# Causal attention and a top-1 GELU mixture in one block that goes chunk by chunk

## The chip, the cores and the metric

The kernel runs on one core of a Trainium2 chip, as one program. The metric is the device time of one execution in microseconds. A core has TensorE (PE in the profile: matrix products; its weight loads are shown as PEld), VectorE (DVE), ScalarE (ACT), GpSimd (POOL) and SyncE (SP), which here issues nearly all DMAs. The engines run independent instruction streams and meet only at semaphores. TensorE's granted clock is given as a share of 2.4 GHz; it has two levels, 1.0 and 0.5 (1.2 GHz). All data of the block that changes are float32 except two small mask operands in bfloat16. A float32 product is recorded as two matmul records with a weight load each, a transpose as one.

## The reference, cut to what matters

The network has four layers of attention-like mixing and feed-forward, on 4096 tokens (8 x 512) of 128 features, each as `x = x + f(layernorm(x))`. The change touches the third layer alone:

```python
def _L2_attn_ref(x, wq, bq, wk, bk, wv, bv, wo, bo):   # H = 64, one head
    q = x @ wq + bq
    k = x @ wk + bk
    v = x @ wv + bv
    w = jnp.einsum('bqh,bkh->bqk', q, k) * scale
    w = w + mask                                       # causal, -1e11 above the diagonal
    w = jax.nn.softmax(w, axis=-1)
    z = jnp.einsum('bqk,bkh->bqh', w, v)
    return z @ wo + bo

def _L2_ffn_ref(x, Wg, bg, W1, b1, W2, b2):            # E = 8 experts of 128
    logits = xf @ Wg + bg
    idx = jnp.argmax(softmax(logits), axis=-1)
    h = gelu(jnp.einsum('th,ehi->tei', xf, W1) + b1, approximate=False)
    y = jnp.einsum('tei,eih->teh', h, W2) + b2
    out = y of the chosen expert, per token
```

The eight sequences of 512 tokens (`B, S = 8, 512`) are independent in the attention; the experts work on each token alone.

## The kernel before, in words

`program` calls one function for each part, each in blocks of its own; all engines meet at the end of a block. The residual x stays on chip as `net.x`, 32 tiles of 128 tokens. A chunk is one sequence, four tiles (`TC = 4`). The third layer runs as a row of blocks:

- `normalise` (L72): sqrt of the variances, then per chunk VectorE normalises four tiles, TensorE turns them, ScalarE copies them to `net.xT`.
- `causal_attention` (L1942): eight loads on SP's queue (L1980); GpSimd adds the output bias to all of x (L1996). The chunk loop is skewed over three chunks by `skewed` (L133): copy of the tokens (L2087), queries (L2008) and keys (L2012) as one product each into one PSUM tile with a copy after each (L2090), values (L2018), four causal rows of scores (L2029), on VectorE mask, maximum and scaling per row (L2124 to L2128), exponential with its sum on ScalarE (L2099), ten transposes of probabilities (L2039) with copies (L2134), the weighted sum with the turned probabilities as weights and the values moving (L2048), division by the sums (L2144), transposes of z (L2067), one more copy, projection (L2072) and the sum into x (L2152).
- `measure` (L156): mean and variance of all 32 tiles.
- `normalise_and_route` (L172): norm, turn, logits for all chunks. Then the choice for all tokens at once (`first_best`, L286) in a block of its own.
- `top1_gelu_products` (L2158): for each chunk the one-hot choice is turned (L2195) and copied twice (L2246, L2247). Expert e gets, before its product (L2207), a product of a mask (L2204) that adds -1e30 where the token has not chosen it, so that the gelu (L2259) gives zero; the down products of all experts and the bias of the chosen one accumulate in PSUM (L2216, L2218). Four PSUM banks `hps` hold up products, and the down products of chunk c-1 stand between those of chunk c. VectorE adds the output (L2268) and measures the tiles for the next layer.

The next layer, `decay_and_mlp` (L2301), is already one block in which steps s overlap the stages of several chunks by an order written out for each engine.

## Time and profile before

| | us |
|---|---|
| median of three runs | 1733.59 (1729.91 to 1737.28) |
| the profiled execution, its own time | 1743.69 |
| its span | 1741.9 |
| TensorE busy in the span | 1396.7 (80%) |
| VectorE busy | 986.0 (57%) |
| ScalarE busy | 788.3 (45%) |
| GpSimd busy | 504.4 (29%) |
| mean granted clock of TensorE | 0.856 |

The span is cut into stages by the blocks above: what an engine does in one of them stands in a window of the trace, not in these totals. A row of the timeline gives the start, the duration, the engine and line, what it writes and reads, and how many instructions are merged; brackets give the idle time before it and who ended it. The profile drops digits from names, so that the causal attention's tiles appear as `a_...`.

### The profile page before, as it was taken

To read this page: it belongs to the slowest core of one execution; us is meant where nothing else is said; L and a number is where in the kernel's file an instruction comes from. 1 tells how busy PE (TensorE), PEld (TensorE's weight loads), DVE (VectorE), ACT (ScalarE), POOL (GpSimd) and SP (SyncE) were. 2 spreads that over 40 slices of the span, in tenths; PEclk is the share of its full clock that TensorE was granted. 3 is DMA by queue.
4 is the path that set the end of the run, shared out by engine and by line. 5 is a ranking of instruction groups with operands and counts; after the bars stand their busy time and mean duration, and the time that the engine had idled before them with its cause. 6 is when DMAs were issued, how large, how long until landed. Compare 5 with 4: busy or idle time off the path is not lost. (4 is left out here: it accounts for less than half of the span.)

```text
span 1741.9 us, 22681 instructions
## 1 busy us (share of the span) xinstructions
PE 1396.7 (80%) x6994; PEld 787.8 (45%) x6994; DVE 986.0 (57%) x2717; ACT 788.3 (45%) x1600; POOL 504.4 (29%) x675
## 2 busy tenths in 40 slices
PE   5899999999952398357998895788589995999587
PEld 1233333333222297123655564355436664777432
DVE  7778888888446565389778533343520014555345
ACT  2567777777730154465664422322043322455344
POOL 4344244432100342855534432100000001321056
PEclk6899999999975599567999897776589996999889
DMA  5111111111052022102243240000000000000001
GB/s 149 41 49 48 43 38 50 53 47 29 11 161 45 20 60 46 33 14 50 51 84 64 50 98 5 0 1 0 1 25 1 1 1 18 1 1 1 2 30 31
DMA packets 75336, 63.24 MB, mean 36 GB/s; under 512 B 19131, under 2 KB 63372, under 8 KB 75220
## 3 DMA queue, kind: packets, MB, share of 16 engines
q1 hardware_dynamic: 71887, 56.13, 13.2%
q0 software_dynamic: 2304, 4.72, 1.1%
q8 instruction: 56, 0.92, 0.2%
q10 hardware_dynamic: 1028, 0.98, 0.2%
q14 instruction: 61, 0.49, 0.1%
HBM read 47.57 MB, written 13.79 MB: 35 GB/s over the span
## 5 line engine op out<-in xcount | busy, mean ns | idle before, releaser
L1060 DVE TENSOR_REDUCE a_nm<-a_aps 128x1 f32<-128x512 f32 x512 | 333.7, 687 | 74.7 <-PE a_aps L825 74.7
L1024 ACT ACTIVATE a_prob<-a_sps 128x512 f32<-128x512 f32 x512 | 271.5, 597 | 114.1 <-PE a_sps L837 113.2
L825 PE MATMUL a_aps<-a_K,a_Q 96*128 96x512 bf16 x512 | 195.6, 402 | 12.6 <-DMA a_K<-k_parts 12.3
L837 PE MATMUL a_sps<-a_Q,a_K 99*128 99x512 bf16 x512 | 156.6, 385 | 1.2 <-ACT a_prob L1024 1.2
L1529 POOL TENSOR_TENSOR p_h<-p_sl,p_t 128x512 f32<-128x512 f32 x72 | 106.5, 1498 | 143.9 <-issue 53.4
L846 PE MATMUL a_ops<-a_prob,a_Vg 128*32 128x512 f32 x1024 | 136.2, 606 | 0.0
L825 PEld LDWEIGHTS a_aps<-a_K,a_Q 96*128 96x128 bf16 x512 | 50.4, 98 | 139.9 <-DVE a_nm L1060 91.3
L1669 ACT ACTIVATE p_sl<-p_up_a 128x512 f32<-128x512 f32 x72 | 42.9, 597 | 110.8 <-PE p_up_b L1559 110.8
L2268 DVE TENSOR_TENSOR x_resid<-x_resid,m2e_yps 128x512 f32<-128x512 f32 x8 | 5.5, 688 | 148.2 <-PE m2e_yps L2218 148.2
L2259 ACT ACTIVATE m2e_h<-m2e_hps,m2e_b 128x512 f32<-128x512 f32 x64 | 43.1, 683 | 96.1 <-PE m2e_hps L2207 95.5
L1559 PE MATMUL p_up_b<-x_normT,p1w_w 128*128 128x512 f32 x144 | 75.9, 609 | 6.7 <-DVE p_t L1777 6.7
L534 POOL CAST a_ms<-a_mr 16x128 bf16<-16x128 f32 x32 | 9.0, 283 | 242.6 <-ACT a_mr L982 242.6
L837 PEld LDWEIGHTS a_sps<-a_Q,a_K 99*128 99x128 bf16 x512 | 50.0, 99 | 61.3 <-ACT a_prob L1024 30.2
L1557 PE MATMUL p_up_a<-x_normT,p1w_w 128*128 128x512 f32 x144 | 74.5, 599 | 2.6 <-ACT p_sl L1669 2.6
L1777 DVE TENSOR_TENSOR p_t<-p_G,p_up_b 128x512 f32<-128x512 f32 x64 | 43.7, 684 | 53.4 <-DMA p_G<-gates_by_expert 25.3
L1567 PE MATMUL p_yps<-p1w_w,p_h 128*128 128x128 f32 x576 | 68.9, 283 | 3.2 <-POOL p_h L1529 3.2
L1567 PEld LDWEIGHTS p_yps<-p1w_w,p_h 128*128 128x128 f32 x576 | 68.1, 199 | 4.4 <-issue 3.2
L1331 ACT ACTIVATE m0e_hT<-m0e_hps,m0e_ws 128x128 f32<-128x128 f32 x160 | 45.7, 368 | 50.6 <-PE m0e_hps L1300 36.2
L2886 PE MATMUL m3e_yps<-m3e_WT,x_normT 128*128 128x512 f32 x128 | 62.7, 629 | 5.4 <-DVE x_resid L2936 5.4
L2218 PE MATMUL m2e_yps<-m2e_W,m2e_h 128*128 128x128 f32 x512 | 65.7, 281 | 0.0
L2207 PE MATMUL m2e_hps<-x_normT,m2e_W 128*128 128x512 f32 x128 | 61.6, 625 | 0.0
L2218 PEld LDWEIGHTS m2e_yps<-m2e_W,m2e_h 128*128 128x128 f32 x512 | 59.6, 191 | 3.9
(515 smaller groups left out, 2780.4 us busy)
## 6 DMA issues: line engine op xcount, KB each, us to landing
p_G<-gates_by_expert SPq DMA_DIRECT2D x32, 512.0 KB
a_Q<-q_parts SPq DMA_DIRECT2D x192, 32.0 KB
a_K<-k_parts SPq DMA_DIRECT2D x31, 96.0 KB
q_parts<-a_partsq SPq DMA_DIRECT2D x7, 384.0 KB, 2.8
k_parts<-a_partsk SPq DMA_DIRECT2D x7, 384.0 KB, 2.8
token_outputs<-m0e_y SPq DMA_DIRECT2D x40, 64.0 KB, 1.5
m0w_w<-in_L_ffn_W SPq DMA_DIRECT2D x1, 2048.0 KB, 9.3
m0w_w<-in_L_ffn_W SPq DMA_DIRECT2D x4, 512.0 KB, 10.1
```

What stands on the lines that cost most here:

```text
L825: nc.tensor.matmul(aps[n % 3][:, :], Q[0:MAX, head, q * P:(q + 1) * P], K[0:MAX, head, :], start=True, stop=True).then_inc(a_ready, 1)
L837: nc.tensor.matmul(sps[(NS * u + k) % 3][:, :], K[0:KB, head, k % TC * P:(k % TC + 1) * P], Q[0:KB, head, :], start=True, stop=True).then_ ...
L846: last = nc.tensor.matmul(ops[32 * j:32 * j + 32, :], Vg[u % 2][:, k, j, :], prob[u % 2][:, j, k, :], start=(k == 0), stop=(k == TC - 1))
L1024: nc.scalar.activation(prob[u % 2][:, k // TC, k % TC, :], sps[n % 3][:, :], ACT.Exp).then_inc(p_done, 1)
L1060: nc.vector.tensor_reduce(nm[u % 2][:, s:s + 1], aps[n % 3][:, :], AX.X, ALU.max, negate=True).then_inc(a_used, 1)
L1529: nc.gpsimd.tensor_tensor(h[c % 2][:, j, :], sl[u % 3][:, :], t[u % 3][:, :], ALU.mult).then_inc(h_done, 1)
L1557: nc.tensor.matmul(up_a[u % 2][:, :], w1[:, j, :], net.xT[:, c * S:(c + 1) * S], start=True, stop=True)
L1559: nc.tensor.matmul(up_b[u % 2][:, :], w3[:, j, :], net.xT[:, c * S:(c + 1) * S], start=True, stop=True).then_inc(up_done, 1)
L1567: last = nc.tensor.matmul(yps[:, k, :], h[c % 2][:, j, k * P:(k + 1) * P], w2[:, j, :], start=(j == 0), stop=(j == NW - 1))
L2207: nc.tensor.matmul(hps[e % 4][:, :], W1[:, e, :], net.xT[:, c * S:(c + 1) * S], start=False, stop=True).then_inc(up_done, 1)
L2218: last = nc.tensor.matmul(yps[c % 2][:, k, :], h[c % 2][:, e, tok], W2[:, e, :], start=False, stop=(e == E - 1))
L2886: last = nc.tensor.matmul(yps[t % 3][:, HALF * q:HALF * (q + 1), :].rearrange("p e d -> p (e d)"), net.xT[:, t * P:(t + 1) * P], WT[:, HAL ...
```

## The change

`normalise`, `skewed`, `measure`, `causal_attention`, `top1_gelu_products` and `moe_top1_gelu` go; one function `causal_and_gelu` with one block takes their place. A step s does the experts of chunk s, the second half of the attention and the routing of chunk s + 1, and the first half of the attention of chunk s + 2, for s from -2 to 8; each engine has its own written order. Further differences:

- `wq` and `wk` lie side by side in one tile of 128 columns and make queries and keys in one product. One copy applies scale (1/8 for queries, 1 for keys) and bias. As the keys then lie on partitions 64 to 127, a DMA on SP's queue moves them to partitions 0 to 63 of `kT` for each chunk.
- The four diagonal masks come first, then four reduces that give the negated maxima; the scaling of the maxima goes.
- Probabilities are turned by key tile into the score banks, copied into four tiles `PT`, and the weighted sum takes the values as weights with 512, 384, 256 and 128 columns moving. It comes out as z transposed, so that the transposes of z and their copy go. Division by the sums happens at the sum into x.
- The value bias goes through `wo` once, at the start (`bc`), and is added to x with the output bias, by chunk, on GpSimd.
- Statistics, root, norm, turn, logits (tokens as weights) and choice are done by chunk.
- The experts have two PSUM banks `hps` instead of four, mask and up product alternate, and there is one bank of `yps`.
- In each step ScalarE runs gelu, square root and exponential.
- `first_best` returns its last instruction, and its closing drain stands at the one remaining caller.

The diff, cut: removed functions are printed above.

```diff
+def causal_and_gelu(nc, net, d):
...
+    SPLACE = ((1, 0), (2, 0), (1, P), (0, 0))
+    PROB = (0, P, 3 * P, 6 * P)
+    TPLACE = ((0, 0), (1, 0), (2, 0), (1, 3 * P))
+    ORDER = (1, 0, 2, 3)
...
+        sps = [p.ps(f"sps{i}") for i in range(3)]
+        tps, ups, yps = p.ps("tps"), p.ps("ups"), p.ps("yps", [P, TC, D])
+        hps = [p.ps(f"hps{i}") for i in range(2)]
...
+        @block.sync
+        def _(sp):
+            sp.dma_start(wqk[:, 0:H], a("wq")).then_inc(qk_loaded, 16)
+            sp.dma_start(wqk[:, H:2 * H], a("wk")).then_inc(qk_loaded, 16)
+            sp.dma_start(qkb[0:H, :], col(a("bq"))).then_inc(qk_loaded, 16)
+            sp.dma_start(qkb[H:2 * H, :], col(a("bk"))).then_inc(qk_loaded, 16)
+            sp.dma_start(wv[:, :], a("wv")).then_inc(v_loaded, 16)
+            sp.dma_start(wo[:, :], a("wo")).then_inc(o_loaded, 16)
+            sp.dma_start(bv[:, :], col(a("bv"))).then_inc(o_loaded, 16)
+            sp.dma_start(bo[:, :], row(a("bo")).to_broadcast([P, D])).then_inc(o_loaded, 16)
+            sp.dma_start(wg[:, :], d["L2_ffn_Wg"]).then_inc(g_loaded, 16)
+            sp.dma_start(bg[:, :], row(d["L2_ffn_bg"]).to_broadcast([P, E])).then_inc(g_loaded, 16)
+            sp.dma_start(W1[:, :, :], d["L2_ffn_W1"].rearrange("e d f -> d e f")).then_inc(e_loaded, 16)
+            sp.dma_start(b1[:, :], d["L2_ffn_b1"]).then_inc(e_loaded, 16)
+            sp.dma_start(W2[:, :, :], d["L2_ffn_W2"].rearrange("e f d -> f e d")).then_inc(e_loaded, 16)
+            sp.dma_start(b2[:, :], d["L2_ffn_b2"]).then_inc(e_loaded, 16)
+            for c in range(B):
+                sp.wait_ge(qk_done, c + 1)
+                wait_for(sp, s_ready, c - 2, TC)
+                sp.dma_start(kT[c % 2][:, :], qk[c % 2][H:2 * H, :]).then_inc(k_moved, 16)
+
...
+            pool.wait_ge(bc_done, 1)
+            for c in range(B):
+                pool.wait_ge(xn1_done, c + 1)
+                xt = net.x[:, tiles(c), :]
+                nc.gpsimd.tensor_tensor(xt, xt, over_tiles(bc[:, :], TC), ALU.add).then_inc(x_biased, 1)
+
+            def queries_and_keys(c):
+                pe.wait_ge(xc_done, c + 1)
+                nc.tensor.matmul(tps[:, :], wqk[:, :], xc[c % 2][:, :], start=True, stop=True).then_inc(qk_ready, 1)
+
+            def scores(c):
+                pe.wait_ge(qk_done, c + 1)
+                pe.wait_ge(k_moved, 16 * (c + 1))
+                wait_for(pe, PT_done, c - 1)
+                for q in ORDER:
+                    bank, off = SPLACE[q]
+                    n = (q + 1) * P
+                    nc.tensor.matmul(sps[bank][:, off:off + n], qk[c % 2][0:H, q * P:n], kT[c % 2][:, 0:n],
+                                     start=True, stop=True).then_inc(s_ready, 1)
+
+            def turn_prob(c):
+                pe.wait_ge(p_done, c + 1)
+                for k in range(TC):
+                    bank, off = TPLACE[k]
+                    for q in range(k, TC):
+                        last = nc.tensor.transpose(sps[bank][:, off + (q - k) * P:off + (q - k + 1) * P],
+                                                   prob[c % 2][:, PROB[q] + k * P:PROB[q] + (k + 1) * P], net.ident[:, :])
+                last.then_inc(p_turned, 1)
+
+            def weigh(c):
+                pe.wait_ge(PT_done, c + 1)
+                pe.wait_ge(v_done, c + 1)
+                wait_for(pe, ohT_done, c - 1)
+                for k in range(TC):
+                    last = nc.tensor.matmul(ups[0:H, k * P:S], V[c % 2][:, k, :], PT[k][c % 2][:, :],
+                                            start=(k == 0), stop=(k == TC - 1))
+                last.then_inc(z_ready, 1)
...
+            def up(c, e):
+                u = E * c + e
+                if u >= 2:
+                    pe.wait_ge(h_done, u - 1)
+                if e == 0:
+                    pe.wait_ge(off_done, c + 1)
+                nc.tensor.matmul(hps[u % 2][:, :], only[:, e, :], off[c % 2][:, :], start=True, stop=False)
+                nc.tensor.matmul(hps[u % 2][:, :], W1[:, e, :], xT[c % 2][:, :], start=False, stop=True).then_inc(up_done, 1)
+
+            def down(c, k):
+                if k == 0:
+                    pe.wait_ge(h_done, E * (c + 1))
+                    pe.wait_ge(ohT_done, c + 1)
+                    wait_for(pe, y_added, c - 1)
+                nc.tensor.matmul(yps[:, k, :], ohT[c % 2][:, tok(k)], b2[:, :], start=True, stop=False)
...
+            pe.wait_ge(bvb_done, 1)
+            pe.wait_ge(o_loaded, 48)
+            nc.tensor.matmul(ups[:, 0:D], bvb[:, :], wo[:, :], start=True, stop=True).then_inc(bc_ready, 1)
+            pe.wait_ge(bc_done, 1)
+            for s in steps:
+                if here(s + 1):
+                    weigh(s + 1)
+                if here(s):
+                    if s == 0:
+                        pe.wait_ge(only_ready, 1)
+                        pe.wait_ge(e_loaded, 64)
+                    up(s, 0)
+                    up(s, 1)
+                if here(s + 1):
+                    project(s + 1)
+                if here(s + 2):
+                    turn_first(s + 2)
+                if here(s):
+                    up(s, 2)
+                    up(s, 3)
+                if here(s + 2):
+                    if s + 2 == 0:
+                        pe.wait_ge(qk_loaded, 64)
+                        pe.wait_ge(v_loaded, 16)
+                    queries_and_keys(s + 2)
+                    values(s + 2)
+                if here(s):
+                    up(s, 4)
+                    up(s, 5)
+                    up(s, 6)
+                if here(s + 2):
+                    scores(s + 2)
+                if here(s):
+                    up(s, 7)
+                    down(s, 0)
+                if here(s + 1):
+                    turn_second(s + 1)
+                if here(s):
+                    down(s, 1)
+                if here(s + 1):
+                    if s + 1 == 0:
+                        pe.wait_ge(g_loaded, 32)
+                    logits(s + 1)
+                if here(s):
+                    down(s, 2)
+                if here(s + 2):
+                    turn_prob(s + 2)
+                if here(s + 1):
+                    turn_choice(s + 1)
+                if here(s):
+                    down(s, 3)
+
...
+            def gelu(c, e):
+                u = E * c + e
+                act.wait_ge(up_done, u + 1)
+                if e == 0:
+                    wait_for(act, y_done, c - 2)
+                nc.scalar.activation(h[c % 2][:, e, :], hps[u % 2][:, :], ACT.Gelu, bias=b1[:, e:e + 1]).then_inc(h_done, 1)
...
+            for s in steps:
+                if here(s + 1):
+                    copy_weighed(s + 1)
+                if here(s):
+                    if s == 0:
+                        act.wait_ge(e_loaded, 64)
+                    gelu(s, 0)
+                    gelu(s, 1)
+                if here(s + 2):
+                    copy_first(s + 2)
+                if here(s):
+                    gelu(s, 2)
+                    gelu(s, 3)
+                if here(s + 2):
+                    copy_queries_and_keys(s + 2)
+                    copy_values(s + 2)
+                if here(s):
+                    for e in range(4, E):
+                        gelu(s, e)
+                if here(s + 1):
+                    root(s + 1)
+                if here(s + 2):
+                    exponentials(s + 2)
+                if here(s + 1):
+                    copy_choice(s + 1)
+
...
+            def maxima(c):
+                wait_for(v, p_done, c - 2)
+                for i, q in enumerate(ORDER):
+                    bank, off = SPLACE[q]
+
+                    v.wait_ge(s_ready, TC * c + (1, 3, 3, 4)[i])
+                    dg = sps[bank][:, off + q * P:off + (q + 1) * P]
+                    tt(dg, dg, mask[:, :], ALU.add)
+                v.drain()
+                for q in ORDER:
+                    bank, off = SPLACE[q]
+                    last = nc.vector.tensor_reduce(nb[c % 2][:, q:q + 1], sps[bank][:, off:off + (q + 1) * P], AX.X, ALU.max,
+                                                   negate=True)
+                last.then_inc(nb_done, 1)
+
...
+            def choose(c):
+                v.wait_ge(lg_ready, c + 1)
+                wait_for(v, oh_turned, c - 2)
+                tt(lg[c % 2][:, :, :], ups[:, 0:TC * E].rearrange("p (t e) -> p t e", e=E), over_tiles(bg[:, :], TC),
+                   ALU.add).then_inc(lg_taken, 1)
+                v.drain()
+                first_best(nc, v, lg[c % 2], m, eq, idx, oh[c % 2], iota, E).then_inc(oh_done, 1)
+
...
+            for s in steps:
+                if here(s - 1):
+                    add_output(s - 1)
+                    measure_second(s - 1)
+                if here(s + 1):
+                    add_attention(s + 1)
+                    measure_first(s + 1)
+                if here(s + 3):
+                    normal_first(s + 3)
+                if here(s + 2):
+                    maxima(s + 2)
+                if here(s + 1):
+                    normal_second(s + 1)
+                    copy_second(s + 1)
+                    if s + 1 == 0:
+                        v.wait_ge(iota_ready, 1)
+                        v.wait_ge(g_loaded, 32)
+                    choose(s + 1)
+                if here(s + 2):
+                    copy_prob(s + 2)
```

```diff
-        causal_attention(nc, net, d)
-        renew_semaphores(nc)
-        moe_top1_gelu(nc, net, d)
+        causal_and_gelu(nc, net, d)
```

## Rows read from the trace of the kernel before

**Rows 1.** Windows: start:end, length, busy (instructions) by engine, TensorE's clock, DMA share, GB/s.
```profile
1066.00:1250.00 184.00, 132.06 (x528) 92.38 (x528) 70.51 (x218) 43.21 (x107) 11.58 (x9) 0.68 0.01 2
1250.00:1289.00 39.00, 18.48 (x88) 8.00 (x88) 20.83 (x110) 15.13 (x23) 2.61 (x3) 0.72 0.10 27
1289.00:1448.00 159.00, 156.20 (x792) 99.37 (x792) 15.39 (x72) 48.25 (x76) 0.00 (x0) 0.98 0.00 1
1289.00:1309.00 20.00, 19.21 (x53) 8.12 (x54) 0.00 (x0) 8.25 (x12) 0.00 (x0) 0.82 0.00 1
1527.00:1609.00 82.00, 76.50 (x470) 61.79 (x469) 45.96 (x141) 40.55 (x88) 16.95 (x13) 0.92 0.00 1
```

**Rows 2.** Waits, 1100 to 1250: who waited for whom, us, times, longest.
```profile
DVE a_sps L2124 <- PE a_sps L2029: 37.8, 7, 8.0
...
PE a_yps L2072 <- DVE a_PT L2134: 17.6, 8, 3.9
```

**Rows 3.** Timeline in the expert products, one half of a chunk, clock 1.0.
```profile
1341.18 1.03 PE L2204 MATMUL m2e_hps<-m2e_off,m2e_only 8*128 8x512 bf16 x4
...
1342.14 3.70 PE L2207 MATMUL m2e_hps<-x_normT,m2e_W 128*128 128x512 f32 x8
...
1343.37 1.49 ACT L2259 ACTIVATE m2e_h<-m2e_hps,m2e_b 128x512 f32<-128x512 f32 x2 [6.25 <-PE m2e_hps L2207]
...
1345.77 0.29 PEld L2216 LDWEIGHTS m2e_yps<-m2e_b,m2e_ohT 8*128 8x128 f32 x2 [0.76 <-ACT m2e_h L2259]
...
1348.17 0.29 PEld L2216 LDWEIGHTS m2e_yps<-m2e_b,m2e_ohT 8*128 8x128 f32 x2
```

**Rows 4.** Timeline: weight loads of short products at high, high and low clock.
```profile
1206.27 0.97 PEld L2072 LDWEIGHTS a_yps<-a_wo,a_PT 128*128 128x128 f32 x8 [2.81 <-DVE a_PT L2134]
...
1269.82 0.42 PEld L245 LDWEIGHTS m_nr_tps<-ident,m_nr_xn 128*128 128x128 f32 x4
...
1231.33 1.83 PEld L2018 LDWEIGHTS a_pj<-a_wv,a_xc 128*128 128x128 f32 x8
```

**Rows 5.** Groups by line, 1080 to 1420: count, busy us, mean ns, idle before.
```profile
L2134 DVE COPY a_PT<-a_tps 128x512 f32<-128x512 f32 (+3 forms) x40 | 20.3, 524 | 18.1 <-PE a_tps L2039 15.0 <-PE a_tps L2067 2.9
...
L2099 ACT ACTIVATE a_prob<-a_sps,a_nb 128x128 f32<-128x128 f32 (+3 forms) x32 | 16.4, 525 | 6.7 <-DVE a_nb L2128 6.6
L2126 DVE TENSOR_REDUCE a_nb<-a_sps 128x1 f32<-128x128 f32 (+3 forms) x32 | 15.7, 492 | 2.4
...
L2124 DVE TENSOR_TENSOR a_sps<-a_sps,a_mask 128x128 f32<-128x128 f32 x32 | 9.4, 295 | 58.2 <-PE a_sps L2029 58.2
...
L227 DVE TENSOR_SCALAR m_nr_xn<-x_resid,x_stat,x_rstd 128x128 f32<-128x128 f32 x32 | 8.7, 341 | 0.3 <-PE m_nr_tps L245 0.2
```

**Rows 6.** Timeline of ScalarE at a table load in the next layer.
```profile
1552.30 0.69 ACT L2603 ACTIVATE d_hb<-d_ups,d_b 128x512 f32<-128x512 f32 x1 [0.17 <-PE d_ups L2506]
1553.01 1.28 ACT L2608 ACT_TABLE_LOAD   x1
1554.30 0.21 ACT L2608 ACTIVATE d_rn<-d_rn 128x8 f32<-128x8 f32 x1
```

**Rows 7.** Timeline: the layer's first instruction, and the attention's loads and bias.
```profile
1066.22 1.28 ACT L120 ACT_TABLE_LOAD   x1 [14.77 <-PEq L58]
...
1081.30 0.36 SPq L1980 DMA_DIRECT2D a_wq<-in_L_attn_wq  x1
...
1085.11 0.44 SPq L1980 DMA_DIRECT2D a_bo<-in_L_attn_bo  x1
...
1088.09 8.81 POOL L1996 TENSOR_TENSOR x_resid<-x_resid,a_bo 128x4096 f32<-128x4096 f32 x1 [4.09 <-DMA a_bo<-in_L_attn_bo]
```

**Rows 8.** Timeline: the layer's last instructions.
```profile
1446.03 0.69 DVE L2268 TENSOR_TENSOR x_resid<-x_resid,m2e_yps 128x512 f32<-128x512 f32 x1 [7.47 <-PE m2e_yps L2218]
...
1447.76 0.38 DVE L2274 BATCH_NORM_AGGREGATE x_stat<-m2e_bst 128x2 f32<-128x6 f32 x4
```

**Rows 9.** DMA issues: size, median us from issue to landing.
```profile
d_mb<-in_L_attn_mlp_b SPq DMA_DIRECT2D x1, 64.0 KB, 4.9
```

More of the change, by code:

```diff
@@ L2252, in _, with copy_weighed @@
[L2252 to L2261 removed]
+            def copy_weighed(c):
+                act.wait_ge(z_ready, c + 1)
+                wait_for(act, o_ready, c - 2)
+                nc.scalar.activation(zT[c % 2][:, :], ups[0:H, :], ACT.Copy).then_inc(z_done, 1)
```

546 lines of the change are left out of this document (190 added, 356 removed).

## The prediction, made before the change was run

> **What bounds the kernel now.** First the windows by stage [rows 1]. The block that changes runs from 1066.2 us, where its first instruction stands [rows 7], to 1448.1, where its last ends [rows 8] (1447.76 + 0.38): 381.9 us. In the attention with its own norm (1066 to 1250) TensorE is busy for 132 of 184 us at a mean clock of 0.68; in the second norm and the routing (1250 to 1289) for 18 of 39 us; in the expert products (1289 to 1448) for 156 of 159 us at 0.98. So the products are bound by TensorE at full clock, and the attention by something else. The waits say what [rows 2]: TensorE waits for VectorE's copy of turned tiles and VectorE for scores, in turns: a chain of one chunk across engines, with too little other work, and half the time at the low clock of 1.2 GHz. What can be gained is the idle time and the low clock of 223 us; nothing in the last 159.
>
> **The change, part by part.** I price a full step of the new pipeline (experts of chunk s, second half of attention of s+1, first half of s+2) at full clock, 2.4 GHz, then its stalls, then the ends.
>
> TensorE's work in a step. Experts: four masks take 0.96 us up to the next product (1341.18 to 1342.14), 0.24 each; four `up` products up to the next weights 3.6, so 0.86 each and a restart; one `down` (nine products) 2.40 (1345.77 to 1348.17) [rows 3]. 8 x (0.24 + 0.86) + 4 x 2.40 = 18.4, and turning the choice 0.5: 18.9. Attention: four transposes 0.42, say 0.5 with their restart, twice: 1.0; eight records of 128x128 float32 weights 0.97, which prices values, projection and logits: 2.9 [rows 4]. Queries and keys in one product of 512 columns: 0.86, as an `up`; before it was two. Scores: 1280 columns at 0.86 per 512: 2.15. Ten transposes of probabilities 1.2. The weighted sum with values stationary: four products with 512 + 384 + 256 + 128 = 1280 columns, again 2.15; before, ten products of 64 columns, whose price is the weights (20 records at 0.12, 2.4): so this edit alone gives 0.3, but it also drops the four transposes of z and their copy from the chain. Sum 10.4. The step is **29.3 us** of TensorE.
>
> The other engines' work is less. VectorE, per chunk: reduces 15.7/8 = 2.0 and mask sums 9.4/8 = 1.2, probability copies (20.3/8 less one of 0.69) 1.85, two norms 2 x 1.1 [rows 5], two statistics of 1.4, the output sum 0.69 (1446.03 to 1447.76 and 0.38 for both) [rows 8], one token copy 0.69, four sums of attention some 1.3, six small routing operations 1.5: about 14. ScalarE: eight gelus of 0.69 [rows 3], exponentials 2.1 [rows 5], five copies and roots 2.6, choice 1.1, and three table loads of 1.28 (gelu, root, exponential in every step): about 15. Neither is the bound by volume; the order decides.
>
> Stalls in the step, by walking the new order of TensorE with these durations from its first product: weigh to 2.15, up 0 and 1 to 4.35, project 5.35, turn_first 5.85, up 2 and 3 to 8.05, queries and keys 8.9, values 9.9, up 4 to 6 13.2, scores 15.35, up 7 16.45, down 0 from 17.55 to 19.95, turn_second 20.7 to 21.2, down 1 23.6, logits 24.6, down 2 27.0, turn_prob 28.2, turn_choice 28.7, down 3 31.1. The waits in it: From an `up` start to its gelu is 1.2 us (1342.14 to 1343.37) and the gelu takes 0.69 [rows 3]. With two banks instead of four, `up(e)` starts after gelu(e-2): 0.24 + 1.23 + 0.69 = 2.16 against two ups of 2.20: just hidden. `down(0)` now stands right behind `up(7)` and waits for its gelu: up ends at 16.45 of the step, gelu at 17.5: stall **1.05**. Behind that gelu on ScalarE's queue stand the table load and the root of s+1 (done 19.1); then VectorE normalises (to 20.6), so `turn_second` waits from 19.95: **0.75**. The exponentials of s+2 have their maxima at 18.1 (scores end 15.35, last mask sum and four reduces), wait for ScalarE until 19.1, load a table and end at 22.6; `turn_prob` stands at 27.0: hidden by 4.4 us; the choice by 1.7, the probability copy (ends 30.4 against 31.1) by 0.7. The values wait for `o_added` (7.0 against 8.9): hidden. The step: 29.3 + 1.8 = 31.1.
>
> The move of the keys to partitions 0 to 63 has no equal in the trace. Copy of queries and keys ends at 9.96, scores stand at 13.2: 3.2 us of cover (values and three ups). Landing of a load after its issue was 3.0 for `bo` (1085.11 to 1088.09) and 4.9 at the long end [rows 7, 9]. I take 2.5 to 3.0, the nearest rows by size, and nothing in the full step; at 4.9 it costs 1.7 a step, 10 us in all; below nothing is excluded, as nothing waits less. The queue of SP holds only the fourteen loads in front of the first move.
>
> Clock. A dense stretch holds it at full (the products). But the next stage of this kernel, built in the same skewed way, was 0.92 on average over four steps [rows 1], with TensorE idle for only 5.5 of 82 us: a clock at half for some 3.3 us of every 20, price 1.6 in a step. I take half of it, 0.9: the new step is denser in long products than that stage. **Step 32.0.**
>
> Tables. After a gelu the load stands at 1553.01, takes 1.28, and the next activation starts at 1554.30 [rows 6]: 1.29 per switch. The Trainium skill (ScalarE: Activation LUTs, What ACT_TABLE_LOAD costs) puts a drain of about 1.38 us on each load, some 2.66 per switch, and advises grouping functions by table, which speaks against this order. This trace shows no such drain.
>
> The ends. From 1066.2: TensorE's first transposes wait for `bc`, which waits for the eighth load. Eight issues took 3.8 + 0.4 us (1081.30 to 1085.11), landing 3.0 [rows 7], then copy, product and sum 1.1: 8.3. Step -2 is one chain, at half clock (eight records 1.83 instead of 0.97 [rows 4]): transposes and copy 1.8, product and copy 2.7, move 2.5, scores 4.3, maxima 2.7, table and exponentials 3.5, transposes 2.1, copies 2.0: 21.6. Step -1: 28.6 (weigh 4.4, z copy and projection 2.9, sum and statistics 2.8, but keys, scores and maxima of chunk 1 stand in front on VectorE until 19.7; then norm, turn, copy, logits, choice, turn, copy 8.9). Six full steps 192.0, and 3 for the clock's rise at their start (the products opened at 0.82 over 20 us [rows 1], 3.6 lost). Step 6: 23.5 of TensorE + 2.0 of stalls = 25.5. Step 7: 18.4 + 1.05 for `down(0)` + 1.2 for a table load ahead of the first gelu = 20.7. Last sum and statistics 2.4. Sum: 8.3 + 21.6 + 28.6 + 192.0 + 3.0 + 25.5 + 20.7 + 2.4 = 302.1, against 381.9: **79.8 us less**. Edits with one answer: the 8.8 us bias sum of GpSimd at the start [rows 7] becomes eight of about 1.3 beside other work, x is biased long before it is needed; first_best's drain moves to its caller, nothing.
>
> The profiled execution took 1743.7 us (span 1741.9): it would take 1663.9. It lies 10.1 above the median of the runs, 1733.6, so the median becomes **1654**.
>
> **The rivals.** *Clean pipeline*: no clock dip, ScalarE's table load ahead of its wait at the ends: 0.9 x 6 + 3.8 less, 1645. For it: products at 1.00. Against: the next stage.
> *The order costs more than I walked*: queues that wait for each other drift apart. The nearest row is TensorE's wait for a VectorE copy in the old attention, 17.6 us over eight chunks, 2.2 each [rows 2]; two such a step, where the probability copy has 0.7 us of cover and the norm none, make 36.4: 6 x 4.4 more, 1680. The late key move (1664) lies inside.
> *A table switch costs twice its load*, 1.3 more each, three in a step: root later by 1.3, gelu(0) done at 6.9 when `up(2)` stands at 5.85 (1.1 more): 2.4 x 6 + 3 for the ends, 1672. Against it [rows 6]. This is about what the rule of the Trainium skill cited above would give.
> *Nothing overlaps*: the order interleaves on paper only, and the old attention with its norm (184/8 = 23.0) and the old products (159/8 = 19.9) stay end to end [rows 1]: 42.9 a step, 6 x 10.9 more, 1719.
> *Slower*: TensorE stays at half clock through the full steps, because short stalls keep recurring. 29.3 of work becomes 58.6, step 60.4, 6 x 28.4 more: 1824. It decides for slower from a step of 45.3 on (32.0 + 79.8/6), that is with the clock at half for more than half of the time. For it: the old attention, which ran at 0.68 although TensorE was busy for 72%. Against: there its waits were 2 to 4 us [rows 2]; the longest now is 1.05.
>
> **How the numbers follow.** Forecast 0.50 (own range 1644 to 1666), clean 0.15, order 0.20, drain 0.05, nothing overlaps 0.03, slower 0.03, still faster than 1640 0.04. The range 1636 to 1688 holds the first four cases with the bounds of the key move and leaves out the rest. About 0.5% is what a measurement of this kernel can tell from no change: faster by more 0.95, within 0.01, slower 0.04 (the slower case, and something unforeseen).
>
> **What the profile will show.** Right: outputs (`add_output`) 31 to 33 us apart in the six full steps, clock at 0.93 or above there, TensorE's longest waits behind gelu 7 and in front of `turn_second`, the table loads 25 of 1.28 us without a gap. Wrong: TensorE waiting for the DMA of `kT` (key move), for `prob` or `PT` at a step's start (order), a clock near 0.5 in the full steps, or first steps far from 22 and 29 us.

## The result and the profile after

The changed kernel took 1658.09 us in the median of four runs (1656.17 to 1661.99), the kernel before beside it 1735.43 (1729.91 to 1739.53): a ratio of 0.9559, 95% interval 0.9526 to 0.9593. Forecast was 1654. The profiled execution took 1657.49 us; its span is 1655.8, its mean granted clock 0.887 (before 0.856).

The windows of the block after the change, cut at the starts of `weigh` (columns as in [rows 1]): steps -2, -1, the six full steps together, steps 6 and 7.

```profile
1056.00:1085.00 29.00, 12.58 (x35) 7.95 (x35) 9.31 (x24) 6.79 (x14) 5.38 (x9) 0.51 0.20 49
1085.00:1115.00 30.00, 21.93 (x64) 13.77 (x64) 11.03 (x41) 8.16 (x17) 1.27 (x1) 0.51 0.02 4
1115.00:1313.00 198.00, 189.62 (x960) 116.90 (x960) 75.60 (x288) 91.41 (x157) 6.34 (x5) 1.00 0.02 5
1313.00:1341.00 28.00, 26.67 (x132) 15.67 (x132) 8.15 (x35) 11.30 (x15) 0.00 (x0) 1.00 0.00 1
1341.00:1364.00 23.00, 20.07 (x95) 11.33 (x93) 3.35 (x18) 5.50 (x8) 0.00 (x0) 1.00 0.00 1
```

Where 223 us of the old stages had TensorE at 0.68 and 0.72 [rows 1], it is now at half clock (0.51) only in the 59 us of the first two steps, and busy for 96% at full clock in the six full ones. The block lasts from 1056.17 (first load) to 1363.93 (1363.55 + 0.38 of the last statistic, against [rows 8]): 307.8 us instead of 381.9, 74.1 less. The two profiled executions differ by more, 86.2 us (1743.69 and 1657.49), and the rest of it lies in parts whose code is the same in both kernels: 10.0 ahead of the block and some 2 behind it. What stands ahead of the block differs between executions: the block began at 1066.2 before, at 1056.2 in this one and at 1068.4 in a later one of the same changed kernel. The medians differ by 77.3, where 79.6 was forecast.

The middle of a full step, from its timeline (start, duration, engine and line; in brackets the idle time before and who ended it):

```profile
1217.92 0.39 PE L2026 MATMUL c_hps<-c_off,c_only 8*128 8x512 bf16 x1
1218.24 1.12 PE L2027 MATMUL c_hps<-c_xT,c_W 128*128 128x512 f32 x2
...
1219.30 1.16 PE L1997 MATMUL c_ups<-c_wo,c_zT 64*128 64x128 f32 x8
...
1225.48 0.46 SPq L1923 DMA_DIRECT2D c_kT<-c_qk  x1
...
1229.53 2.42 PE L1973 MATMUL c_sps<-c_kT,c_qk 64*128 64x256 f32 x8
...
1231.88 0.39 PE L2026 MATMUL c_hps<-c_off,c_only 8*128 8x512 bf16 x1
...
1233.36 0.69 ACT L2104 ACTIVATE c_h<-c_hps,c_b 128x512 f32<-128x512 f32 x1 [3.04 <-PE c_hps L2027]
1234.07 1.28 ACT L2127 ACT_TABLE_LOAD   x1
1234.10 0.48 PE L2034 MATMUL c_yps<-c_b,c_ohT 8*128 8x128 f32 x2 [0.78 <-ACT c_h L2104]
...
1235.36 0.30 ACT L2127 ACTIVATE c_std<-x_stat,eps_col 128x4 f32<-128x4 f32 x1
1235.68 1.28 ACT L2137 ACT_TABLE_LOAD   x1
...
1237.12 0.66 PE L2004 MATMUL c_tps<-ident,c_xn 128*128 128x128 f32 x4 [0.55 <-DVE c_xn L2238]
```

A mask and its `up` product take from 1217.92 to 1219.30, 1.38 us, where the forecast, from four masks in a row and four ups in a row [rows 3], had 1.10. The scores take 2.35 (1229.53 to 1231.88). TensorE has two real waits, 0.78 for the last gelu and 0.55 for the norm. The key move is issued at 1225.48, four microseconds ahead of the scores; it lands 2.3 us later, as the table of DMA issues says (size, median us from issue to landing):

```profile
c_kT<-c_qk SPq DMA_DIRECT2D x8, 128.0 KB, 2.3
```

The ledger of the block, in us:

| | predicted | measured |
|---|---|---|
| start to the first transposes | 8.3 | 8.4 |
| step -2 | 21.6 | 20.4 |
| step -1 | 28.6 | 30.4 |
| six full steps, with the clock's rise | 192.0 + 3.0 | 197.7 (32.96 each) |
| step 6 | 25.5 | 27.2 |
| step 7 | 20.7 | 21.5 |
| last sum and statistics | 2.4 | 2.1 |
| block | 302.1 | 307.8 |

The total missed by 5.7 us, and 2.7 of it lies in the full steps. But a step of 32.96 where 32.0 was forecast is right for partly wrong reasons: the forecast held 0.9 for a dip of the clock, and there was none (clock 1.00); its stalls were 1.8 and are 1.3 by the profile's idle time, which begins at the modelled end of the product before, or 1.6 by the distances of starts. So the work itself is larger by 2.0 to 2.3 us a step. The experiments ask what that is, and which part of the change brought the gain.

### The profile page after: what moved, and what is told of

It is laid out like the page before. It is cut to its first block and busy times, and to the rows that moved or that the text cites. A ratio compares the mean times of both kernels' runs of the same rounds, so it can differ in the third digit from the quotient of the medians.

```text
span 1655.8 us, 22037 instructions
## 1 busy us (share of the span) xinstructions
PE 1350.8 (82%) x6868; PEld 746.3 (45%) x6868; DVE 984.1 (59%) x2722; ACT 804.6 (49%) x1604; POOL 503.6 (30%) x678
## 5 line engine op out<-in xcount | busy, mean ns | idle before, releaser
L2027 PE MATMUL c_hps<-c_xT,c_W 128*128 128x512 f32 x128 | 72.0, 645 | 0.0
L2104 ACT ACTIVATE c_h<-c_hps,c_b 128x512 f32<-128x512 f32 x64 | 43.9, 687 | 53.6 <-PE c_hps L2027 53.5
L1945 POOL TENSOR_TENSOR x_resid<-x_resid,c_bc 128x512 f32<-128x512 f32 x8 | 10.2, 1271 | 189.0 <-DVE c_xn L2184 183.8
L2036 PE MATMUL c_yps<-c_W,c_h 128*128 128x128 f32 x512 | 65.7, 281 | 0.0
L2036 PEld LDWEIGHTS c_yps<-c_W,c_h 128*128 128x128 f32 x512 | 59.6, 191 | 3.9
```

The source lines that it names most:

```text
L2027: nc.tensor.matmul(hps[u % 2][:, :], W1[:, e, :], xT[c % 2][:, :], start=False, stop=True).then_inc(up_done, 1)
L2036: last = nc.tensor.matmul(yps[:, k, :], h[c % 2][:, e, tok(k)], W2[:, e, :], start=False, stop=(e == E - 1))
```

## The experiments

Each was run beside the kernel before, which took 1746 us there (medians 1745.94 to 1746.09) and not 1735, so ratios and steps are compared. A run without a ratio is a single one, and is read from the steps of its profile more than from its time. The edits are shown against the changed kernel, cut at `...`. A step is the distance of two starts of `weigh`.

**The changed kernel again**, beside the experiments on weighted sum and bias.

> This is the changed kernel itself, beside the next three on one chip, so that they have their neighbour to be compared with. Both theories on the masks, and both on the weighted sum, expect the ratio to the kernel before at 0.953 to 0.959, full steps of 32.9 to 33.0 us and a block of 307 to 309 us.

1667.45 us, ratio 0.9536 (0.9495 to 0.9577); block 306.8 us, steps 32.96 but for one of 33.82, in which the clock was at half for 3.4 us. So a dip of the kind priced at 0.9 for every step came in one of twelve full steps that two profiles show, and cost 0.86 there.

**What the pair of mask and up product pays for.** Three theories: the 8 rows of the mask's weights between products of 128 rows; the change from bfloat16 to float32 and back; or the waits for two PSUM banks.

```diff
-        only = p.sb("only", [E, E, P], BF)
+        only = p.sb("only", [P, E, P], BF)
-        ohT, off, h = two("ohT", [S], E), two("off", [S], E, BF), two("h", [E, S])
+        ohT, off, h = two("ohT", [S], E), two("off", [S], P, BF), two("h", [E, S])
...
+            for i in range(2):
+                nc.gpsimd.memset(off[i][:, :], 0.0)
...
+                act.wait_ge(only_filled, 1)
...
-                nc.scalar.activation(off[c % 2][:, :], ups[0:E, :], ACT.Copy, bias=-1.0).then_inc(off_done, 1)
+                nc.scalar.activation(off[c % 2][0:E, :], ups[0:E, :], ACT.Copy, bias=-1.0).then_inc(off_done, 1)
```

> The mask product of each expert (weights of 8 rows, bfloat16) gets weights and data of 128 rows, rows 8 to 127 zero; nothing else changes. In the changed kernel a pair of mask and up product takes 1.37 us where I priced 1.10, eight times a step. Theory rows: weights that fill only 8 rows aren't loaded beside the running product of 128 rows, and the gap of about 0.1 on entering and 0.17 on leaving comes from that. It expects 1.10 to 1.15 a pair, steps of 30.9 to 31.2 instead of 32.96 and a block of about 291 us instead of 307.7: the median near 1641. Theory type: the gap comes from the switch between float32 and bfloat16: 1.37 a pair, 1658. Theory wait: the gap comes from the wait for a gelu that stands ahead of each mask product: 1.37, 1658.

1644.45 us, ratio 0.9425 (0.9393 to 0.9456), step 30.78, block 285.1 us. Its timeline:

```profile
1215.06 1.02 PE L2029 MATMUL c_hps<-c_xT,c_W 128*128 128x512 f32 x2 [0.16 <-issue]
1215.92 0.38 PE L2028 MATMUL c_hps<-c_off,c_only 128*128 128x512 bf16 x1
1216.14 1.02 PE L2029 MATMUL c_hps<-c_xT,c_W 128*128 128x512 f32 x2
```

With sixteen times the rows, 15 of 16 zero, the mask takes 0.22 us up to the next product (1215.92 to 1216.14) instead of 0.32 (1217.92 to 1218.24 above), and an `up` takes 0.86 up to the next product (1215.06 to 1215.92) instead of 1.06 (1218.24 to 1219.30): a pair of 1.08 instead of 1.38. The step is 2.18 shorter with the same types and the same two banks, so type and banks are not the cause. (The block is 21.7 shorter than that of the changed kernel again, but 3.2 of this stand in step -1, which has no expert product, and 0.9 are the dip.)

How the rows cost shows in the weight loads (PEld): first those of the changed kernel at 1217.92, then those of this run.

```profile
1217.92 0.09 PEld L2026 LDWEIGHTS c_hps<-c_off,c_only 8*128 8x128 bf16 x1 [0.76 <-issue]
1218.24 0.30 PEld L2027 LDWEIGHTS c_hps<-c_xT,c_W 128*128 128x128 f32 x2 [0.23 <-issue]
...
1215.49 0.10 PEld L2028 LDWEIGHTS c_hps<-c_off,c_only 128*128 128x128 bf16 x1 [0.24 <-issue]
1215.92 0.41 PEld L2029 LDWEIGHTS c_hps<-c_xT,c_W 128*128 128x128 f32 x2 [0.33 <-issue]
```

With 128 rows the mask's weights are loaded 0.43 us ahead of its product (1215.49 for 1215.92) and those of the `up` 0.22 ahead (1215.92 for 1216.14), while the product before still runs. With 8 rows among 128 each load starts only when its own product does (1217.92, 1218.24): it no longer overlaps. The wait for the gelu stands ahead of the mask in both.

Without the mask products altogether (the output is then not the reference's, as every expert adds its part):

```diff
-                nc.tensor.matmul(hps[u % 2][:, :], only[:, e, :], off[c % 2][:, :], start=True, stop=False)
-                nc.tensor.matmul(hps[u % 2][:, :], W1[:, e, :], xT[c % 2][:, :], start=False, stop=True).then_inc(up_done, 1)
+                nc.tensor.matmul(hps[u % 2][:, :], W1[:, e, :], xT[c % 2][:, :], start=True, stop=True).then_inc(up_done, 1)
```

> The mask products are left out, so that every expert adds to every token (the choice of one expert isn't computed in the mixture). The waits for the gelu stay, now ahead of the up product. Theories rows and type: nothing but float32 products of 128 rows follow each other, 0.86 a pair, unless the gelu of two before now binds: its chain is 0.86 + 0.3 + 0.69 = 1.85 for two, so up to 0.93. Step 32.96 - 8 x 0.45 = 29.4. Theory wait: the wait alone costs about 0.19 each, 1.05 a product, step 30.4.

Step 29.47 (time 1639.83): eight masks cost 3.5 us a step as written, 0.44 each. By the run before the product has 0.22 and the mixing of row counts 0.27 (2.18 for eight). That is 0.05 more than found: without masks the `up` products themselves stand beside weights of 64 rows or columns, and take 0.96 there (two from 1212.96 to 1214.88) instead of 0.86. The theory of waits, at 30.4, falls.

The other side of it, 8 rows in float32 (`only` and `off` without `BF`):

> The mask operands keep their 8 rows but become float32, as the products next to them: two records of 512 columns instead of one. A pair of float32 records with 128 rows takes 0.86 us. Theory that the 8 rows cost (0.27 a pair, by the run with 128 rows): a pair of mask and up product takes 0.86 + 0.86 + 0.27 = 2.0, so the pair is 0.6 above the 1.37 of the changed kernel, a step of about 38. Rival, that the change of type between bfloat16 and float32 cost the 0.27: 1.72 a pair, a step of about 35.8.

1756.66 us. The clock was at half for 20.5 us in each of two steps (47.4) and for 10.2 in each of two others (42.8); the two steps at full clock take 38.83 (1257.29 to 1296.12 is one). Masks and ups of its timeline:

```profile
1259.59 1.12 PE L2026 MATMUL c_hps<-c_off,c_only 8*128 8x512 f32 x2
1260.64 1.12 PE L2027 MATMUL c_hps<-c_xT,c_W 128*128 128x512 f32 x2
1261.69 1.12 PE L2026 MATMUL c_hps<-c_off,c_only 8*128 8x512 f32 x2
```

Two products of one type, alternating between 8 and 128 rows, take 1.05 each instead of 0.86: a pair of 2.10 where rows predicted 2.0 and type 1.72. The cost is 0.19 for each product, with no change of type at all; the step of 38.8 is the 38 of this theory, not the 35.8 of the other.

Beside the masks the chosen bias, too, has 8 rows (`ohT`, `b2`); padded to 128 like the masks:

> The masks and, beside them, the chosen bias of the experts get operands of 128 rows, of which 120 are zero. With the masks alone at 128 rows the step was 30.78 us. If short weights cost wherever they stand between long ones, the four biases in a step (two records each) should give back 0.1 to 0.2 each as well: a step of 30.1 to 30.4 us, the block 2.5 to 4 us shorter than with the masks alone. Rival, that only the alternation with bfloat16 masks cost: a step of 30.8 and no gain.

1640.99 us, ratio 0.9394 (0.9356 to 0.9432), step 29.73: 1.05 less than with the masks alone, where 0.4 to 0.7 was expected. The bias's share reads in the timeline: it took 0.41 (1359.38 to 1359.79 in the changed kernel) and takes 0.23:

```profile
1263.25 0.39 PE L2039 MATMUL c_yps<-c_b,c_ohT 128*128 128x128 f32 x2
1263.48 1.95 PE L2041 MATMUL c_yps<-c_W,c_h 128*128 128x128 f32 x16
```

The whole 1.05 can be found in the two timelines. Three `down`s with their biases are 0.79 shorter together (`down(1)` takes 2.01, 1263.25 to 1265.26, instead of 2.30), and the pieces ahead of these biases 0.27, their last product being followed by weights of its own height. What the first `down` gains goes into the wait for the norm behind it, 0.74 instead of 0.55.

Of the block's gain the kernel did not keep all: the block is 8.8 us shorter than with the masks alone (276.4), the time 3.5. In the profiles, 3.0 of the difference stands ahead of the block (its start, 1069.0 against 1066.0, in the same code), and 1.7 behind it. There the next layer began at a granted clock of 0.53 over its first 47 us, against 0.67 in the other run:

```profile
1346.00:1393.00 47.00, 29.95 (x118) 23.27 (x119) 22.00 (x64) 17.20 (x36) 13.73 (x19) 0.53 0.07 17
```

**The key move.** A second DMA behind the first doubles it.

```diff
+                sp.dma_start(kT[c % 2][:, :], qk[c % 2][H:2 * H, :]).then_inc(k_first, 16)
+                sp.wait_ge(k_first, 16 * (c + 1))
                 sp.dma_start(kT[c % 2][:, :], qk[c % 2][H:2 * H, :]).then_inc(k_moved, 16)
```

> The DMA that moves the keys is done twice, the second after the first has landed. One takes 2.3 us from issue to landing; in a full step it is issued 11.2 us after the step's start and the scores stand 4.05 us after the issue, so 1.75 us of cover are left. Theory cover: the second needs 2.35 more, so 0.6 a step shows as a wait of the scores (6 x 0.6 = 3.6), and in steps -2 and -1, where nothing covers the move, 2.35 each: 8.3 us in all, block 316. Rival (moves are free): no change. Rival (queues drift): over 2 us a step, block over 325.

1673.05 us, block 318.2 (316 expected). The second DMA is issued 2.2 us behind the first (1238.41 against 1236.19), 1.75 of it were covered, and 0.44 are left as the scores' idle time: TensorE waits only for what the cover does not reach, as both the cover and the price of the forecast had it. But only the second and third full step (33.5 each) are near the 33.4 that this makes. The first has 35.4, its first 4 us at half clock, and from the fourth on the steps are 34.3:

```profile
1240.75 2.39 PE L1976 MATMUL c_sps<-c_kT,c_qk 64*128 64x256 f32 x8 [0.44 <-issue]
...
1245.29 0.48 PE L2037 MATMUL c_yps<-c_b,c_ohT 8*128 8x128 f32 x2 [0.78 <-ACT c_h L2107]
1245.70 3.45 PE L2039 MATMUL c_yps<-c_W,c_h 128*128 128x128 f32 x16
```

The sixteen records of one `down` take 3.45 instead of 2.05: TensorE is at half clock for 3.4 us, once in each of these steps, at the same place behind the two waits. Here the clock's dip of the forecast is real, at 0.86 a step, in three of six steps; over the last five (1158 to 1329) TensorE is busy for 164 of 171 us. The wait of 0.44 alone does not decide it: two steps have it and no dip, and one step of the changed kernel had a dip without it. What decides is open.

The other way is to have no move: queries and keys in two products of 64 columns of weights, each into partitions 0 to 63 with a copy of its own; `keys` stands behind up 4.

```diff
-                nc.tensor.matmul(tps[:, :], wqk[:, :], xc[c % 2][:, :], start=True, stop=True).then_inc(qk_ready, 1)
+                nc.tensor.matmul(tps[0:H, :], wqk[:, 0:H], xc[c % 2][:, :], start=True, stop=True).then_inc(qk_ready, 1)
+
+            def keys(c):
+                pe.wait_ge(q_done, c + 1)
+                nc.tensor.matmul(tps[0:H, :], wqk[:, H:2 * H], xc[c % 2][:, :], start=True, stop=True).then_inc(qk_ready, 1)
...
-                sp.dma_start(kT[c % 2][:, :], qk[c % 2][H:2 * H, :]).then_inc(k_moved, 16)
```

> One part of the change undone: queries and keys in two products of 64 output rows and with two copies, the second product behind up product 4, the keys copied straight to their place and no DMA. Expected by my prices: one product more of 0.86 us on TensorE in each full step (32.96 to 33.8, 5.2 us), ScalarE's second copy of 0.68 hidden; in steps -2 and -1 the 2.3 us of the move go and a product of 1.9 and a copy of 0.7 come: 0.3 more each. Block 313.5. Rival (the edit brings nothing because TensorE has gaps): 308. Rival (the copy in ScalarE's queue delays the gelus, so more than the product): over 316.

1671.91 us, steps of 34.30 (33.8 expected), one of 35.17 with a clock dip and the first one 36.05, its first 3.6 us at half clock. Each product takes 1.00 up to the next start, more than the one product with 128 columns of weights (0.86, 1223.62 to 1224.48 in the changed kernel); its weights, too, are loaded only when it starts (1198.36):

```profile
1198.37 1.07 PE L1955 MATMUL c_tps<-c_xc,c_wqk 128*64 128x512 f32 x2
1199.37 1.10 PE L1964 MATMUL c_ups<-c_wv,c_xc 128*128 128x64 f32 x8
```

So queries and keys as one product are worth 1.3 us a step, 8 in the block, and the move that they need is hidden.

**The weighted sum.** Values moving again: ten products with the turned probabilities as weights, a copy, four transposes behind up 0 and a second copy.

```diff
-                for k in range(TC):
-                    last = nc.tensor.matmul(ups[0:H, k * P:S], V[c % 2][:, k, :], PT[k][c % 2][:, :],
-                                            start=(k == 0), stop=(k == TC - 1))
+                for q in range(TC):
+                    for k in range(q + 1):
+                        last = nc.tensor.matmul(ups[:, H * q:H * (q + 1)], PT[k][c % 2][:, tok(q - k)], V[c % 2][:, k, :],
+                                                start=(k == 0), stop=(k == q))
...
+            def turn_weighed(c):
+                pe.wait_ge(zc_done, c + 1)
+                for k in range(TC):
+                    last = nc.tensor.transpose(ups[0:H, tok(k)], zc[:, k, :], net.ident[:, :])
...
```

> Undoes one part, the weighted sum with the values stationary: ten products with the turned probabilities as weights and 64 columns of values moving, a copy of z, four transposes of z behind up 0 and a second copy. Theory that the part is worth its work on TensorE and little more: 20 records at 0.12 us are 2.4 against the 2.30 measured, and the transposes add 0.5, so a full step is 0.6 longer (33.6 us), the lone chains at the ends 1.5 to 3 together, and the time 5 to 7 us above the changed kernel's. Rival, the chain: the copy of z now stands ahead of gelu 0 and the second copy ahead of gelu 1, and with two PSUM banks up 2 waits for them: 1.0 to 1.5 more in each step, a step of 34.5 to 35.0 and 11 to 15 us above. Rival, nothing: the step stays within 0.2 of 32.96, because other queues set it.

1680.51 us, ratio 0.9618 (0.958 to 0.9657), 13.1 above the changed kernel beside it; the block is 12.7 longer (319.5 against 306.8). The time is that of the chain theory, its mechanism is not: the full step is 33.28, only 0.32 longer, nearer to the theory of work (33.6) than to 34.5. The rest lies at the start: step -1 is 3.2 longer (1.4 against the first profile of the changed kernel) and the first full step 8.3 (1128.51 to 1169.80 for its `weigh` starts). Its window:

```profile
1128.00:1170.00 42.00, 40.16 (x179) 24.73 (x179) 11.42 (x44) 15.83 (x28) 1.26 (x1) 0.80 0.02 4
```

The granted clock there is 0.80, and TensorE is busy for 40.2 of 42 us: the clock was at half for 17 us and rose for good 19 us into this step, where in the changed kernel it stood at 1.0 in the whole of it. This is the "clock's rise" of the forecast, which had put 3.0 on it; whether it is caused by the longer step -1 or by what TensorE does in it, the run does not tell.

**Is it the interleaving?** First the same work with each chunk's expert products in one piece, and the gelus behind one another. The order of TensorE in a step, in short, first as it was, then as edited:

```diff
-   up(s, 0..1)  project  turn_first  up(s, 2..3)  queries_and_keys  values  up(s, 4..6)  scores
-   up(s, 7)  down(s, 0)  turn_second  down(s, 1)  logits  down(s, 2)  turn_prob  turn_choice  down(s, 3)
+   project  turn_first  queries_and_keys  values  scores  turn_second  logits  turn_prob  turn_choice
+   up(s, 0..7)  down(s, 0..3)
```

> All instructions and buffers of the changed kernel, but in each step TensorE and ScalarE do the experts of chunk s behind the attention and routing pieces instead of between them. Theory cover: the gain comes from expert products standing where the attention's chain waits. Then a step is the chain of attention and routing (weigh 2.3, copy and projection 2.1, turn, copy, product, copy 4.3, move 2.4, scores and maxima 4.9, norm, turn, copy, logits 4.0, choice, turn, copy 3.5: 23 at full clock, some 26 where it falls) and then 21.4 of experts: 44 to 48 us a step, a clock well below 1.0, block 385 to 405, about the time of the kernel before the change. Rival edits: the smaller amount of work (one product for queries and keys, values stationary, no passes over all chunks) carries the gain: steps under 38, block under 340.

1760.58 us against 1745.94 for the kernel before; steps of 45.8 to 47.9, block 401.4 us. Windows of two of its steps, and one step's TensorE:

```profile
1217.00:1263.00 46.00, 36.98 (x164) 22.28 (x162) 13.00 (x50) 15.09 (x26) 1.26 (x1) 0.85 0.02 3
1263.00:1310.00 47.00, 38.94 (x159) 23.39 (x159) 13.00 (x50) 15.18 (x26) 1.26 (x1) 0.78 0.01 3
```

```profile
1227.11 3.91 PE L1973 MATMUL c_sps<-c_kT,c_qk 64*128 64x256 f32 x8 [2.35 <-issue]
1234.46 1.12 PE L2004 MATMUL c_tps<-ident,c_xn 128*128 128x128 f32 x4 [3.43 <-DVE c_xn L2213]
```

One block and step by step, but with nothing to cover the waits: they are 2 to 3.4 us, as in the old attention [rows 2], and the clock falls with them (scores 3.91 instead of 2.42). One product, stationary values and no transposes of z are all in it, and it is no faster than before. So together they bring no gain in this order: what brings it is that the waits are covered.

Second, the step with the expert work left out (up, down and mask products, gelus and the sum of outputs; the output is not the reference's):

> The up and down products, gelus and their sum into x are left out (the mixture's output isn't computed); the order of the rest is as it was. Theory cover: attention and routing alone are a chain of one chunk, as in step -1, which took 30.4 us: steps of 25 to 31 us with the clock near 0.5 to 0.6, only 2 to 8 us less than the 32.96 with 20.6 us of expert products in them. Rival (TensorE's work is all that counts): 11 to 14 us of work, steps under 20 us.

1597.35 us; steps of 25.4 to 28.9.

```profile
1117.00:1279.00 162.00, 110.19 (x384) 70.19 (x384) 71.07 (x283) 50.27 (x102) 6.32 (x5) 0.62 0.03 5
```

The attention and routing alone need 27.1 us a step in the mean, at a clock of 0.62, where their work at full clock was priced at 10.9 (10.4 and 0.5 for turning the choice). The experts' is 8 x 1.37 + 4 x 2.39 = 20.5. End to end that makes 47.6, near the grouped order's 46.7 in the mean; interleaved it is 33.0.

**What the readings suggest.** The waits before `down(0)` and `turn_second` go if `up(7)` stands ahead of the scores, and VectorE does its second norm ahead of the maxima:

```diff
                     up(s, 6)
+                    up(s, 7)
                 if here(s + 2):
                     scores(s + 2)
                 if here(s):
-                    up(s, 7)
                     down(s, 0)
...
+                if here(s + 1):
+                    normal_second(s + 1)
                 if here(s + 2):
                     maxima(s + 2)
                 if here(s + 1):
-                    normal_second(s + 1)
```

> Two moves in the order: TensorE does up product 7 ahead of the scores, so that they stand between it and down 0, and VectorE does the second norm ahead of the maxima. Theory stalls: the two waits of a full step go (0.85 in front of down 0, 0.55 in front of turn_second) and nothing else gets late (exponentials end about 3 us ahead of turn_prob): steps of 31.5 to 31.7 instead of 32.96, step 6 unchanged or 0.5 less, block 299. Rival (the later scores make the copy of the tokens or the exponentials late): 32.5 or more.

1660.73 us (1745.94 before). The step is 31.34, 1.62 less, somewhat more than expected, but for the first full one of 33.66, its first 5 us at half clock; the profile shows no idle time of TensorE in it (its ends are modelled):

```profile
1157.00:1313.00 156.00, 156.00 (x797) 96.69 (x796) 62.41 (x246) 76.03 (x130) 5.07 (x4) 1.00 0.02 5
```

All of it together (masks and bias with 128 rows, this order, and the product for `bc` behind the first values instead of ahead of the first transposes):

> Together: masks and the bias of the down products with 128 rows (zeros in rows 8 to 127), the order of i_scores_late, and TensorE starts with the turn of chunk 0 instead of waiting for the bias of the attention, whose product moves to a free bank behind the first values. By theory rows: pair of mask and up 1.07, bias product 0.25 instead of 0.41 and no gap around it (0.7 a step), stalls 1.4 a step, start 4.2: steps 32.96 - 2.2 - 0.7 - 1.4 = 28.7, block about 4.2 + 20.4 + 29 + 172 + 23.5 + 19 + 2 = 270 instead of 307.7, ratio to the kernel before 0.934. If the shorter pairs make the gelus late (2.14 us for two pairs against 2.05 for product and gelu), 29.5 a step.

1626.95 us (1621.81 to 1629.49), ratio 0.9323 (0.9302 to 0.9345): faster than both kernels, 0.9536 and 0.9559 being the ratios of the changed one. Its step is 28.02, its block 265.8 us. The last part gave less than expected: the first transposes start 5.6 us after the block does instead of 8.4 (4.2 expected), and the first `weigh` only 1.2 us earlier than before.

## Why the prediction was right, point by point

- *What bounds.* Right. The old attention's chain was the gain to be had, and the experts the cover: the grouped order gives all of it back.
- *The step's work, 29.3.* The mis-sized term is the pair of mask and `up`: 1.10 from rows in which four of a kind stand in a row [rows 3], 1.37 in the alternation that the change itself brings. Eight pairs are 2.2 us a step, 13 in six, and the runs show the cause: 8 rows between 128, whose weights are not loaded beside the running product. The smaller ones: scores 2.35 and the weighted sum 2.30 for 2.15 each, with weights of 64 rows or columns next to others of 128; the attention's listed terms add up to 10.3, not 10.4; project 1.08, values 0.93 and logits 0.88 sum to the 2.9 forecast; one `down` 2.39 for 2.40, turning probabilities 1.1 for 1.2.
- *Stalls, 1.05 and 0.75.* Right in place and order: 0.78 behind gelu 7, as the waits of the full steps below say (total, times, longest), and 0.55 behind the norm. Most of the difference lies in how they are counted. By starts, `down(0)` stands 2.22 behind the mask of `up(7)` (1231.88 to 1234.10), where 1.10 + 1.05 was forecast, and `turn_second` 3.02 behind `down(0)`, where 2.40 + 0.75 was. The length of the pairs has no part in it: in the run with masks of 128 rows the waits are 0.78 and 0.55 again.

```profile
PE c_yps L2034 <- ACT c_h L2104: 4.7, 6, 0.8
```

- *The clock, 0.9 a step and 3.0 for its rise.* Not there: 1.00 in all six steps, and already so in the first. The row it was taken from, the next stage, had such dips; the double move, in three of six steps, and one step of the changed kernel's second profile show that this pipeline has them too. The two errors, 2.2 too little and 0.9 too much, cancelled in part: without its 0.9 x 6 + 3.0 for the clock the sum would have been 14 us short instead of 5.7.
- *The key move.* 2.3 us where 2.5 to 3.0 was taken; hidden in the full steps with 1.75 to spare, in step -2, where it was counted, 1.67 of it is open:

```profile
1071.85 4.60 PE L1973 MATMUL c_sps<-c_kT,c_qk 64*128 64x256 f32 x8 [1.67 <-DMA c_kT<-c_qk]
```

- *Table loads.* 25 of them, as forecast, 1.28 each without a gap (1234.07 and 1235.68 above). The rival of a drain beside each load falls. By the rule cited from the Trainium skill (ScalarE: Activation LUTs, What ACT_TABLE_LOAD costs) a switch would have taken some 2.66; in this trace the next activation starts 1.29 after the load does (1234.07 to 1235.36), so measurement decides against it here.
- *Values stationary, 0.3 alone, and the transposes.* The products cost the same either way, 2.30 stationary and 2.27 moving (1236.36 to 1238.63 in that run): the 0.3 is wrong. What the part gives in a full step, 0.32, comes from the transposes that go. The 11 us at the start were not foreseen.
- *The ends.* Step -1 is 30.4 for 28.6, and that is the clock: with the same instructions in this step it took 28.7 at a mean granted clock of 0.58 in the second profile, and 25.4 at 0.73 in the four runs that change masks and bias, against 0.51 here. That 28.6 came near is then partly luck. So is the end of the sum: the profiled execution was forecast at 1663.9 and took 1657.49 although its block was 5.7 longer than forecast, as the parts around the block were 12 shorter in it than before. Steps 6 and 7 are 1.7 and 0.8 long by the same pairs (8 x 0.27 each, less what the stalls gave).
- *The rivals.* Clean pipeline (1645): its mechanism came, its time did not, for the pairs filled its place. Order costs more (1680): TensorE's waits in the step are 1.3, not 6.2. Nothing overlaps (1719): no, outputs are 32.96 apart, inside 31 to 33. Slower, from a step of 45.3 on: not here, but the grouped run with steps of 45.8 to 47.9 came out at 1760.58 against 1745.94, which fits the turning point, though by waits (TensorE idle for 8 to 9 of 46 us) as much as by the clock, which was at 0.78 to 0.85 and not at half.

## What to carry over

A price from a run of equal instructions does not hold where a new order alternates them: read it from rows in which two kinds follow each other, or bound it upwards. A short operand padded with zeros to the height of its neighbours can be cheaper than one of its true size: here 26 us of 1667, for a few memsets (19 in the six full steps and 7 in the last two by the profiles; the block gained 4 more in step -1 and a dip, which the zeros do not explain). And in a pipeline by steps look at each moved chain for what covers it: the same instructions were 1667 us interleaved and 1761 grouped.

## What the hardware showed that was not expected

- Products whose weights have 8 rows and 128 rows in turns cost more than either kind in a row: 1.05 for 0.86 each in float32, 0.3 a pair with the 8 rows in bfloat16. With rows alike the next weights are loaded up to 0.43 us ahead of their product, beside the running one. After each change of rows (among 8, 64 and 128) in the full steps, the load starts within 0.01 us of its own product. For a change of columns the runs show both: queries in two products have no load ahead (1198.36 and 1198.37), the transposes of z, with 64 columns, have it 0.43 ahead.
- The clock dips for 3.4 us inside dense steps: in three of six in the double move, where TensorE was busy for 96%, in one of twelve full steps of the changed kernel, and not in the full steps of the runs with 128 rows.
- Step -1, with the same instructions, took 25.4, 28.7 and 30.4 us in six profiles, at a granted clock of 0.73, 0.58 and 0.51. When the clock then stayed at half into the first full step, as in the run with values moving, it cost 8 us more: a difference larger than the edit's 0.32 a step.
